# Norms returned from DRAM in one transfer of 128 rows of 4 KB instead of four transfers of 1 KB rows

## The reference

```python
x = x + attention(layernorm(x))            # 16 heads of 64, causal penalty -50
y = layernorm(x)
for i in range(6):
    y = attn_layer(shift_tokens(y), Wqkv[i], q_scale[i], k_scale[i], Wo[i]) + y
    y = ffn_layer(shift_tokens(y), ...) + y
x = x + y

def attn_layer(...):                        # the part that the change touches
    q = l2norm(q) * q_scale                 # per head: divide by the norm over 64 channels
    k = l2norm(k) * k_scale
    q, k = rotary(q), rotary(k)
    out = local_attention(q, k, v)          # windows of 32, each looks one window back
```

## Time and profile before

| | us |
|---|---|
| median of 3 runs | 2100.08 (2099.58 to 2102.47) |
| the profiled execution, its own time | 2099.16 |
| its span | 2097.3 |
| TensorE busy | 2029.8 (97%), 23760 matmuls |
| VectorE busy | 1501.0 (72%) |
| ScalarE busy | 1330.2 (63%) |
| GpSimd (POOL) busy | 1453.3 (69%) |
| POOL's idle time before L857 | 213.8 |
| mean DMA rate | 98 GB/s |

### The profile page before, as it was taken

How to read it: one execution, slowest core, us unless ns; L and a number is a source line. 1 busy time by engine, 2 the same in 40 slices (tenths; PEclk the granted TensorE clock), 3 DMA queues, 4 the chain that set the end, 5 groups by cost and what they waited for, 6 DMA issues and landing times.

```text
span 2097.3 us, 61286 instructions
## 1 busy us (share of the span) xinstructions
PE 2029.8 (97%) x23760; PEld 1292.7 (62%) x23760; DVE 1501.0 (72%) x3291; ACT 1330.2 (63%) x2522; POOL 1453.3 (69%) x1439
## 2 busy tenths in 40 slices
PE   8999999998689999999999999999999999999997
PEld 4555555554456666666666666666666666666654
DVE  5666666665677777777877777877777877777853
ACT  5666666665356567666667676667666667666654
POOL 3344443433678888878877888878977888878852
PEclk9999999999799999999999999999999999999999
DMA  4000000000444554455454464454644455444441
GB/s 134 6 1 6 1 1 6 1 1 6 109 108 123 144 151 110 123 129 159 124 127 110 127 175 117 119 126 126 172 120 107 122 139 160 121 121 118 120 109 28
DMA packets 218416, 204.96 MB, mean 98 GB/s; under 512 B 32403, under 2 KB 211601, under 8 KB 218129
## 3 DMA queue, kind: packets, MB, share of 16 engines
q1 hardware_dynamic: 218128, 201.04, 37.1%
HBM read 83.53 MB, written 13.63 MB: 46 GB/s over the span
## 4 chain that ended last, share of the span: by engine, by line
SPq 25%; POOL 20%; DMA 14%; PE 12%; issue 3%; ACT 0%; DVE 0%; DVEq 0%; ACTq 0%; POOLq 0%
POOL T L857 20%; DMA RB<-norms 14%; SPq L876 10%; SPq L850 8%; SPq L870 7%; PE bank L891 3%; PE bank L779 3%; PE bank L1109 1%; PE bank L918 1%; PE bank L990 1%; PE bank L965 1%; PE bank L1131 1%; PE bank L813 1%; PE bank L912 0%; PE bank L1010 0%
## 5 line engine op out<-in xcount | busy, mean ns | idle before, releaser
L857 POOL TENSOR_TENSOR T<-T,RB 128x512 f32<-128x512 f32 x384 | 480.4, 1285 | 213.8 <-DMA RB<-norms 213.8
L805 POOL TENSOR_TENSOR T<-T 128x512 f32<-128x512 f32 x384 | 491.7, 1283 | 78.4 <-DVE T L800 78.0
L891 PE MATMUL bank<-WU,XT 128*32 128x512 f32 x3072 | 414.3, 599 | 2.0 <-ACT U L898 1.9
L779 PE MATMUL bank<-XT,WQK 128*128 128x256 f32 x1536 | 401.0, 394 | 14.7 <-DVE T L800 13.1
L539 POOL TENSOR_SCALAR PR<-PR,RI 128x512 f32<-128x512 f32 x256 | 174.1, 694 | 291.0 <-DVE RI L439 289.9
L785 ACT ACTIVATE SQ<-bank 128x512 f32<-128x512 f32 x384 | 224.9, 600 | 237.4 <-PE bank L779 236.9
L779 PEld LDWEIGHTS bank<-XT,WQK 128*128 128x128 f32 x1536 | 277.2, 192 | 136.3 <-issue 68.5
L799 DVE TENSOR_TENSOR T<-bank,TAB 128x512 f32<-128x512 f32 x384 | 261.8, 682 | 124.5 <-ACT SQ L785 67.6
L898 ACT ACTIVATE U<-bank 128x512 f32<-128x512 f32 x384 | 228.8, 596 | 96.4 <-PE bank L891 95.8
L363 ACT ACTIVATE PR<-PR,NM 128x512 f32<-128x512 f32 x256 | 183.5, 718 | 147.1 <-DVE NM L434 145.7
L800 DVE TENSOR_TENSOR T<-bank,TAB 128x512 f32<-128x512 f32 x384 | 261.2, 680 | 0.0
(11 more groups left out here) (124 smaller groups left out, 3059.0 us busy)
## 6 DMA issues: line engine op xcount, KB each, us to landing
RB<-norms SPq DMA_DIRECT2D x384, 128.0 KB, 3.3
KZ<-T SPq DMA_DIRECT2D x384, 128.0 KB, 2.5
QP<-T SPq DMA_DIRECT2D x192, 256.0 KB, 4.7
TAB<-rotary_dram SPq DMA_DIRECT2D x24, 512.0 KB, 5.2
norms<-RN SPq DMA_DIRECT2D x96, 128.0 KB, 1.7
WQK<-wqk_halves_dram SPq DMA_DIRECT2D x12, 512.0 KB, 6.2
WVS<-wv_turned_dram SPq DMA_DIRECT2D x29, 128.0 KB, 3.4
WOS<-wo_lanes_dram SPq DMA_DIRECT2D x29, 128.0 KB, 3.5
```

What stands on the lines that cost most here:

```text
L779: m = pe.matmul(b[:, ab * HALF:(ab + 1) * HALF], WQK[n % 3][:, i, ab, :], XT[s % 2][:, hf * HALF:(hf + 1) * HALF], start=True, stop=True)
L805: pool.tensor_tensor(t1, t1, T2[i % 2][:, ::-1, :], ALU.add).then_inc(l_rotated.sem, 1)
L857: pool.tensor_tensor(t1, t1, RB[:, i:i + 1, :].to_broadcast([P, 2, HALF]), ALU.mult).then_inc(l_scaled.sem, 1)
L891: i = pe.matmul(bank[1][h * WIN:(h + 1) * WIN, :], XT[s % 2][:, c0:c0 + WIN], WU[:, lp * HG + h, :], start=True, stop=True)
```

## The change

The DRAM buffer gets another layout: 32 rows (h) of 4 KB, in which the four parts g stand one behind the other. RN is written into it so that the 1 KB of partition 32g + h goes to row h, place g. The return is one transfer: the first four rows, each repeated for 32 partitions, into the 4 KB of each of the 128 partitions of RB. The waits on s_rb count 16 a front instead of 64. Lines behind L849 have numbers that are smaller by one.

```diff
-            norms = [nc.dram_tensor(f'norms{i}', (P, HALF), F32).ap() for i in range(2)]
+            norms = [nc.dram_tensor(f'norms{i}', (WIN, HG * HALF), F32).ap() for i in range(2)]
...
             def sp_norms_out(f):
                 sp.wait_ge(l_newton.sem, l_newton.at(f))
                 if f >= 2:
-                    sp.wait_ge(s_rb, 64 * (f - 1))
-                sp.dma_start(norms[f % 2], RN[:, :]).then_inc(s_rn, 16)
+                    sp.wait_ge(s_rb, 16 * (f - 1))
+                sp.dma_start(norms[f % 2].rearrange('h (g c) -> g h c', g=HG), RN[:, :]).then_inc(s_rn, 16)
 
             def sp_norms_in(f):
                 sp.wait_ge(s_rn, 16 * (f + 1))
                 sp.wait_ge(l_scaled.sem, l_scaled.at(f - 1))
-                rows = norms[f % 2].rearrange('(g h) (a c) -> h a g c', h=WIN, a=1)
-                for h in range(HG):
-                    sp.dma_start(RB[h * WIN:(h + 1) * WIN, :, :], rows[h].to_broadcast([WIN, HG, HALF])).then_inc(s_rb, 16)
+                rows = norms[f % 2][0:HG, :].rearrange('h (a q) -> h a q', a=1).to_broadcast([HG, WIN, HG * HALF])
+                sp.dma_start(RB[:, :, :].rearrange('p g c -> p (g c)'), rows).then_inc(s_rb, 16)
 
             def pool_scale(f, i):
                 if i == 0:
-                    pool.wait_ge(s_rb, 64 * (f + 1))
+                    pool.wait_ge(s_rb, 16 * (f + 1))
```

More of the change, by code:

```diff
@@ L1457, in sp_layers_program @@
                 sp.wait_ge(s_rn, 16 * FRONTS)
-                sp.wait_ge(s_rb, 64 * FRONTS)
+                sp.wait_ge(s_rb, 16 * FRONTS)
                 sp.wait_ge(s_kz, 128 * 2 * STEPS)
```

## The result

The changed kernel takes 2428.95 us (median of 6 runs, 2415.82 to 2431.38), the kernel before beside it 2103.11 us: a ratio of 1.1544, 95% interval 1.1516 to 1.1571. It is slower by some 326 us.

A forecast was written before the change was run, and what follows sets the result against it. It took a ring without slack (POOL's scaling, SP's relayout issues, the norms' return) as the bound, not TensorE; +3.1 us a slot times 96 slots, +291 us on 2099, gave 2390 us, range 2295 to 2500.

The forecast's parts named there:

- The ring and its lack of slack: POOL scaling, SP's relayout issues, RB return and landing: 15.76 us a slot; any change of the return passes one for one.
- Four engines, by the smaller leading count: The one return transfer, 4 DRAM rows into 128 partitions, runs on 4 DMA engines, not 16; all sizes together 84%.
- The W2S transfer of 113 rows: Load at L1041, DMA share 0.07 at 22 GB/s: taken as running on one engine, so engines get equal leading steps.
- The price: Return on 4 engines: mean 9.0 us against 5.9, +3.1 us a slot, times 96 slots: +291 us.
- the term for KZ: Return after the KZ relayout: one issue 0.44 + fixed 2.35 + transfer 5.3 = 8.1 us, against 6.3 before.
- less company than sixteen: Reason for taking 5.3 us for the return's 512 KB on four engines, with 6.0 and 7.3 as slower ends.
- What I cost at nothing: Transfer out on 4 engines, later loads, POOL's other work and TensorE (83% of a slot) add no time.
- come up to 5 us later: Shift of X, table and weight loads queued behind RB come up to 5 us later, with a slot or more to spare.
- with 16 engines: Rival: the return runs on sixteen engines, mean 5.1 us, until TensorE stops the gain: 2082 us. Chance 7%.
- The clock: Rival: TensorE's idle time gathers at a wait for KZ and QP, its clock falls: 2560 us. Chance 6%.
- the price that I gave the rival: Half clock for 20 us makes TensorE the bound: +3.6 us in two slots, 48 times, 170 us on top.
- The signs: RB lands after some 8 us, share about 0.25, POOL's wait some 500 us, landing about 45% of chain, TensorE about 85%.

The follow-up runs named there:

- The dose runs: four_4kb_on16 with the source's repeat of 32 rewritten so that its leading count is 8, 4 or 2: 2175.0, 2404.7 and 2864.7 us.
- after_later_loads: Changed kernel with the table and weight loads issued behind the transfer out of the norms, not right behind the return: 2390.9 us.
- the doubled sums: TensorE makes the sums of squares twice: changed kernel 2435.07 us (without 2428.95), kernel before 2167.25, four_4kb_on16 2165.98 (without 2088.82).
- four_4kb_on16: Changed kernel's layout and transfer out, but the return is four transfers of one 4 KB row, each repeated for 32 partitions: 2088.82 us, ratio 0.9925 to the kernel before.
- copies2_on8: Changed kernel with each row stored twice in DRAM by four small transfers out; one return reads 8 rows, each repeated 16 times: 2284.8 us, ratio 1.0864 to the kernel before.

## Why the prediction was right

**The ring and its lack of slack**: right. The same pieces stand in the chain after, and 3.52 us a slot of return gave 3.39 us a slot of time. The dose runs show it again at three more sizes.

**Four engines, by the smaller leading count**: right, and now shown by itself. The W2S transfer of 113 rows was a sound guide, though it had equal counts on both sides.

**The price**: the sum was 291 us against 326 in the medians (2428.95 less 2103.11). The mean return of before was 5.97 us (I had 5.9); the new one 9.49 (I had 9.0). By kind, after QP it was 10.03 us where I had 9.9, after KZ 8.99 where I had 8.1: the term for KZ is the one that was too small. I reckoned it as a fixed part and the four engines' best rate, 5.3 us, "less company than sixteen". The company came: without table and weight loads behind it the return after KZ took 8.46 us, with them 9.37. `after_later_loads` takes 38 us away and brings the return after KZ to 8.39. It stands at 2390.9 us, on the sum's 2390, which had left such company out, but that close a match is partly luck: its return is still 0.3 us longer than reckoned after KZ (8.39 and 8.1) and 0.1 us shorter after QP (9.79 and 9.9).

**What I cost at nothing**: TensorE was no bound, shown by the doubled sums, though it was busy 87% of the time from 600 to 2300 us, not 83% of a slot. The transfer out cost nothing with the return on 16 engines (`four_4kb_on16`), and little that can be seen on 4: in the changed kernel, after QP and without loads behind, 21 returns without a transfer out issued beside them took 9.41 us, and 11 with one took 9.73. After KZ it is issued within 45 of the 48 returns, so there it was not parted. I had written that loads behind the return "come up to 5 us later"; what they cost was not their own lateness but the return's.

**The rivals**: with 16 engines the kernel is indeed bound by TensorE; I had 2082 us for it and `four_4kb_on16` has 2089. The clock did fall, to a mean of 0.95. The place was another than I said. TensorE's instructions in order of time (start us, us, and the idle time before with what ended it):

```profile
1020.12 1.02 PE L1108 MATMUL bank<-XNT,W1S 128*114 128x512 f32 x2
1024.91 1.00 PE L964 MATMUL bank<-ident,PL 128*128 128x128 f32 x4 [3.77 <-POOL PL L954]
```

And the sum of these waits from 600 to 2300 us (us, times, longest):

```profile
PE bank L964 <- POOL PL L954: 209.0, 80, 5.9
```

TensorE does not wait for KZ and QP at the scores but for the normalised probabilities (L964 on L954), 209 us in 80 waits, since they stand behind L856 in POOL's queue. In the stretch with this 3.77 us wait and in the one behind it the clock is at the lower level, 1.2 GHz, for a part of the time, as the busy times of three stretches of 10 us show (clock third from last):

```profile
1016.00:1026.00 10.00, 6.23 (x91) 4.12 (x84) 5.87 (x12) 5.32 (x8) 9.58 (x8) 0.95 0.34 75
1026.00:1036.00 10.00, 10.00 (x123) 6.49 (x123) 7.29 (x15) 5.51 (x11) 4.55 (x5) 0.88 0.34 100
1036.00:1046.00 10.00, 8.82 (x110) 5.02 (x111) 7.12 (x14) 4.73 (x9) 9.85 (x10) 1.00 0.44 104
```

The lower clock stayed short of the price that I gave the rival, and all of its cost fell into time that TensorE had over.

**The signs**: the share of 0.25, the return as the largest part of the chain (48% of the stretch, I had 45%) and POOL's wait (598.7 us, I had some 500) came as said. RB landed some 9 to 10 us after SP began its issue, where I had 8.1 and 9.9. TensorE is busy 88% of the span, not 85%; a part of its work runs at the lower clock.

## What to carry to other kernels

Before merging transfers, look at what stands in front of both access patterns: four rows repeated 32 times over into 128 partitions kept twelve of sixteen engines idle, and the three issues saved were no match for it. When a transfer stands in a ring without slack, its length goes into the time once a turn; look for that ring in the chain of waits even if another engine is busy 99%. Where the ring has to be shortened, keep a leading count that all 16 engines can share (16 and 32 did it here) and lengthen the rows instead: here four transfers of one 4 KB row each, 0.75% faster than the kernel before.

## What the runs showed of the hardware that was not expected

- A transfer on four engines is slowed by loads issued behind it: after QP 9.64 us in the mean without table or weight loads behind it, 11.45 us with them.
- Four engines reading rows of 1 KB moved 96 GB/s (median) with the four rows side by side in DRAM and 76, at times 41, with the rows 4 KB apart, at the same share; 110 us between the two kernels. Why is open.
- One transfer on 8 engines (`copies2_on8`) returns in 7.91 us, four on the same number in 6.78. Why is open.
- The issue of the return grew as well: 0.44 us the median for one of the four before, 0.68 for the one now; the transfer out, written as 4 by 32 rows, 0.58 in place of 0.34 us.
